# Second graph layer: the linear attention's fold put beside the last 20 groups of edges, and its finish regrouped over seven and two tiles

## What is computed

```python
xn = _layernorm(x, axis=-1)
x = x + _L1_gnn_ref(xn, edge_index, ...) + _L1_mix_ref(xn[None], ...)[0]

# _L1_gnn_ref, the end of it
denom = jax.ops.segment_sum(ex, dst, num_segments=N)
alpha = ex / (denom[dst] + 1e-16)
out = jax.ops.segment_sum(h[src] * alpha[:, :, None], dst, num_segments=N)
return out.reshape(N, H * C) + bias

# _L1_mix_ref: 8 heads of 64
q, k, v = ...          # xn @ w_qkv; k and v normalized per head
dots = jnp.einsum('bhnd,bhne->bhde', k, v)
out = jnp.einsum('bhnd,bhde->bhne', q, dots) * (1.0 / n)
return out @ w_out + b_out
```

## Time and profile before

| | us |
|---|---|
| median of 3 runs | 4831.45 (4831.15 to 4832.38) |
| the profiled execution | 4826.72 |
| its span in the trace | 4825.0 |
| `Stage2`, first DMA issue to the copy's end | 2046.85 to 3200.92 |
| `fold1`, to the first work of `finish1` | to 3219.79 |
| `finish1`, to the end of its last operation | to 3300.94 |

### The profile page before, as it was taken

The page is one execution under the profiler, slowest core; times in us unless marked ns, Lnnn a source line. Parts: engine busy times, 40 slices in busy tenths (PEclk is TensorE's granted clock), DMA queues, the critical chain, the costliest instruction groups (busy, mean ns, idle before and its releaser), DMA issues. The chain is left out here.

```text
span 4825.0 us, 68016 instructions
## 1 busy us (share of the span) xinstructions
PE 3819.0 (79%) x17730; PEld 2381.1 (49%) x17730; DVE 3259.6 (68%) x10150; ACT 2202.3 (46%) x3971; POOL 2816.7 (58%) x2922
## 2 busy tenths in 40 slices
PE   7478789999999999768888888764448888878776
PEld 6344456656665566534444444443424444444444
DVE  7667274645546455488888888876566777777777
ACT  4123222233323223356666666620346666666665
POOL 0355376656656420077777777730477777777775
PEclk9999799999999999989999999886568889998888
DMA  1232311111111100344444444531222222222221
GB/s 60 54 88 64 99 46 34 42 34 37 41 30 40 23 16 1 126 125 138 140 137 136 139 140 140 138 91 32 64 34 39 40 40 44 41 39 40 39 38 28
DMA packets 277159, 323.15 MB, mean 67 GB/s; under 512 B 78502, under 2 KB 232004, under 8 KB 276796
## 3 DMA queue, kind: packets, MB, share of 16 engines
q0 software_dynamic: 105328, 175.77, 16.5%
q1 hardware_dynamic: 171468, 143.20, 10.1%
HBM read 288.85 MB, written 29.89 MB: 66 GB/s over the span
## 5 line engine op out<-in xcount | busy, mean ns | idle before, releaser
L2716 POOL DMA_INDIRECT st_rows<-tabr,router_rsrc x1072 | 1022.2, 954 | 334.7 <-issue 322.1
L1392 POOL DMA_INDIRECT st_rows<-tab,graph_gsrc x748 | 741.8, 992 | 499.8 <-PE st_pe L1415 299.0
L2134 POOL DMA_INDIRECT all_XT<-tab,graph_gsrc x880 | 867.6, 986 | 272.2 <-issue 252.5
L1645 ACT ACTIVATE st_h<-st_ph,st_shift,st_scale 128x448 f32<-128x448 f32 x448 | 324.4, 724 | 757.4 <-PE st_ph L1503 757.2
L2164 PE MATMUL st_po<-all_XT,st_hot 128*128 128x264 f32 x1760 | 579.6, 457 | 84.2 <-DVE gat_sum L2317 83.0
L2317 DVE TENSOR_TENSOR gat_sum<-gat_sum,st_po 128x264 f32 x880 | 376.5, 428 | 143.5 <-DVE gat_sum L2317 75.4
L2164 PEld LDWEIGHTS st_po<-all_XT,st_hot 128*128 128x128 f32 x1760 | 297.5, 204 | 288.1 <-DVE gat_sum L2317 176.3
L2761 PE MATMUL st_px<-all_XT,st_w 128*128 128x512 f32 (+1 forms) x832 | 424.0, 659 | 10.7 <-ACT st_hid L2821 10.7
L1732 DVE TENSOR_TENSOR gcn_acc<-gcn_acc,st_pe 128x65 f32 x748 | 166.3, 222 | 381.7 <-PE st_pe L1415 290.7
L2773 PE MATMUL st_py<-st_w,st_hid 128*128 128x256 f32 x1568 | 422.5, 416 | 0.5 <-ACT st_hid L2821 0.5
L2734 PE MATMUL st_pad<-st_adr,st_hott 128*128 x1072 | 121.1, 183 | 346.4 <-DVE st_zd L2887 325.4
(11 more groups left out here) (489 smaller groups left out, 7233.4 us busy)
## 6 DMA issues: line engine op xcount, KB each, us to landing
st_bc<-drowr SPq DMA_DIRECT2D x268, 128.0 KB
st_bc<-drow SPq DMA_DIRECT2D x220, 128.0 KB
st_rows<-tabr,router_rsrc POOLq DMA_INDIRECT x1072
all_XT<-tab,graph_gsrc POOLq DMA_INDIRECT x880
xtd<-tab_xt SPq DMA_DIRECT2D x98, 128.0 KB, 1.9
st_rows<-tab,graph_gsrc POOLq DMA_INDIRECT x748
tab<-gat_sum SPq DMA_DIRECT2D x7, 924.0 KB
all_XT<-xtd SPq DMA_DIRECT2D x49, 128.0 KB
```

The source lines that it names most:

```text
L1392: g.indirect_dma_start(self.rows[:, b, u, :], None, self.R.tab0, bass.IndirectOffsetOnAxis(self.R.gsrc[:, t:t + 1], 0)).then_inc(self.s_ro ...
L1645: a.activation((self.h1, self.h2)[l][:, fb, h * HALF:(h + 1) * HALF], self.ph[:, m % 3, 0:HALF], ACT.Relu, bias=self.shift[:, l, i:i + 1], ...
L2134: g.indirect_dma_start(self.rows[:, b, u, :], None, self.R.tab1, bass.IndirectOffsetOnAxis(self.R.gsrc[:, t:t + 1], 0)).then_inc(self.s_ro ...
L2716: g.indirect_dma_start(self.rows[:, b, u, :], None, self.R.tabr, bass.IndirectOffsetOnAxis(self.R.rsrc[:, t:t + 1], 0)).then_inc(self.s_ro ...
```

## The change

Three things. The fold moves from a phase of its own into `Stage2`, in five steps tied to the loop steps q = 200 (`FOLD`) to 204: DVE copies `pacc` and masks it (step 0), PE multiplies with `wout` (1), DVE copies the product in two operations (2), PE multiplies with `wqt` (3), DVE copies `weff` (4). Its weights are loaded by SP, behind the row of group 200 and behind a wait for the last `keys`, since they take the place of `wkv`; its mask is made by POOL ahead of the first gather of the stage. `fold1` is gone. `finish1` works with longer operations: the product with the reciprocals and the two additions that don't need PE over seven tiles at a time, the addition of the matmul's result over two tiles; it has four PSUM banks of two tiles and three feature buffers, and loads the features of the first iteration before the biases.

```diff
@@ -2027,6 +1976,7 @@
     HALFKV = KV // 2
     FEAT = GH * GC
     PAIRS = HALFKV // P
+    FOLD = 4 * (W + 1)
...
+        K = self.PAIRS
+        old = self.wkv.rearrange("p c n -> p (c n)")
+        self.wqt = old[:, 0:K * D].rearrange("p (k d) -> p k d", k=K)
+        self.wout = old[:, K * D:2 * K * D].rearrange("p (k d) -> p k d", k=K)
+        old = self.kc.rearrange("p k n -> p (k n)")
+        self.m1 = old[:, 0:K * D]
+        self.bd = old[:, K * D:K * D + K * P].rearrange("p (k e) -> p k e", k=K)
+        self.kvsum = old[:, K * D + K * P:K * D + 2 * K * P]
+        assert 2 * K * D <= C * self.KV and K * D + 2 * K * P <= 2 * self.KV
+        self.diag = f.sb("diag", [P, P])
...
@@ -2121,10 +2083,15 @@
             n, b = divmod(q, 4)
             if b == 3 and n + 1 < W:
                 features(n + 1)
+            if q == self.FOLD:
+                s.wait_ge(self.s_kvp, 2 * W)
+                s.dma_start(self.wqt, rows(self.A.m1_wqt)).then_inc(self.s_fw, 16)
+                s.dma_start(self.wout, rows(self.A.m1_wout)).then_inc(self.s_fw, 16)
 
 
 
     def pool(self, g):
+        block_mask(g, Steps(g, self.s_mask), self.diag, HC1)
         for q in range(self.GROUPS):
...
+        def fold(step):
+            K = self.PAIRS
+            if step == 1:
+                t.wait_ge(self.s_fw, 32)
+                t.wait_ge(self.s_bd, K)
+                for k in range(K):
+                    bank = (self.pkv, self.pacc)[k // 2]
+                    mm = t.matmul(bank[:, k % 2 * D:(k % 2 + 1) * D], self.bd[:, k, :], self.wout[:, k, :],
+                                  start=(k % 2 == 0), stop=False, skip_group_check=True)
+                mm.then_inc(self.s_pm, 1)
+            if step == 3:
+                t.wait_ge(self.s_m1, 2)
+                for m in range(C):
+                    for k in range(K):
+                        mm = t.matmul(self.pkv[:, m * D:(m + 1) * D], self.wqt[:, k, m * P:(m + 1) * P],
+                                      self.m1[:, k * D:(k + 1) * D], start=(m == 0 and k == 0), stop=False,
+                                      skip_group_check=True)
+                mm.then_inc(self.s_pw, 1)
...
             scores(q + 3)
             if b == 3 and 1 <= n <= W:
                 outer(n - 1)
+            if q > self.FOLD:
+                fold(q - self.FOLD)
...
+        def fold(step):
+            K = self.PAIRS
+            if step == 0:
+                v.wait_ge(self.s_kv, W)
+                v.tensor_copy(self.kvsum, self.pacc[:, :]).then_inc(self.s_kvs, 1)
+                v.wait_ge(self.s_kvs, 1)
+                v.wait_ge(self.s_mask, 3)
+                for k in range(K):
+                    v.scalar_tensor_tensor(self.bd[:, k, :], self.kvsum[:, k * P:(k + 1) * P], 1.0 / N, self.diag[:, :],
+                                           ALU.mult, ALU.mult).then_inc(self.s_bd, 1)
+            if step == 2:
+                v.wait_ge(self.s_pm, 1)
+                v.tensor_copy(self.m1[:, 0:2 * D], self.pkv[:, :]).then_inc(self.s_m1, 1)
+                v.tensor_copy(self.m1[:, 2 * D:4 * D], self.pacc[:, :]).then_inc(self.s_m1, 1)
+            if step == 4:
+                v.wait_ge(self.s_pw, 1)
+                v.tensor_copy(R.weff[:, :, :].rearrange("p c d -> p (c d)"), self.pkv[:, :])
...
@@ -2380,8 +2386,8 @@
                 variance(n - 1)
             if b == 2 and 1 <= n <= W:
                 weigh_values(n - 1)
-        v.wait_ge(self.s_kv, W)
-        v.tensor_copy(R.kvsum[:, :], self.pacc[:, :])
+            if q >= self.FOLD:
+                fold(q - self.FOLD)
...
         den = f.sb("den", [P, W, GH])
-        xt = f.sb("xt", [P, 2, TPI, C, P])
-        po = f.ps("po", [P, 2, 512])
-        s_x = [f.sem(f"x{k}") for k in range(2)]
-        s_w, s_st, s_o, s_m, s_b, s_a, s_m2 = (f.sem(n) for n in ("w", "st", "o", "m", "b", "a", "m2"))
+        xt = f.sb("xt", [P, 3, TPI, C, P])
+        po = f.ps("po", [P, 4, 2, D])
...
             @block.sync
             def _(s):
-                s.dma_start(bias[:, 0, :], spread(A.gat_bias[0])).then_inc(s_w, 16)
-                s.dma_start(bias[:, 1, :], spread(A.m1_bout[0])).then_inc(s_w, 16)
                 for i in range(ITER):
-                    if i >= 2:
-                        s.wait_ge(s_o, TPI * (i - 1))
-                    s.dma_start(xt[:, i % 2].rearrange("p j c t -> p j (c t)"),
-                                R.xtd[TPI * i:TPI * (i + 1), :, :].rearrange("j p d -> p j d")).then_inc(s_x[i % 2], 16)
+                    if i >= 3:
+                        s.wait_ge(s_o, TPI * (i - 2))
+                    s.dma_start(xt[:, i % 3].rearrange("p j c t -> p j (c t)"),
+                                R.xtd[TPI * i:TPI * (i + 1), :, :].rearrange("j p d -> p j d")).then_inc(s_x[i % 3], 16)
+                    if i == 0:
+                        s.dma_start(bias[:, 0, :], spread(A.gat_bias[0])).then_inc(s_w, 16)
+                        s.dma_start(bias[:, 1, :], spread(A.m1_bout[0])).then_inc(s_w, 16)
 
             @block.tensor
             def _(t):
-                for i in range(ITER):
-                    t.wait_ge(s_x[i % 2], 16 * (i // 2 + 1))
-                    for j in range(TPI):
-                        n = TPI * i + j
-                        if n >= 2:
-                            t.wait_ge(s_b, n - 1)
+                for k, ns in enumerate(pairs):
+                    if k >= 4:
+                        t.wait_ge(s_b, k - 3)
+                    for n in ns:
+                        i, j = divmod(n, TPI)
+                        if j == 0:
+                            t.wait_ge(s_x[i % 3], 16 * (i // 3 + 1))
                         for c in range(C):
-                            mm = t.matmul(po[:, n % 2, 0:D], xt[:, i % 2, j, c], R.weff[:, c, :], start=(c == 0),
-                                          stop=(c == C - 1))
+                            mm = t.matmul(po[:, k % 4, n - ns[0], :], xt[:, i % 3, j, c], R.weff[:, c, :],
+                                          start=(c == 0 and n == ns[0]), stop=False, skip_group_check=True)
                         mm.then_inc(s_o, 1)
 
             @block.vector
             def _(v):
                 st = Steps(v, s_st)
 
+                def scale(i):
+                    a = R.gat[:, TPI * i:TPI * (i + 1), 0:GH * GC].rearrange("p t (h c) -> p t h c", c=GC)
+                    d = den[:, TPI * i:TPI * (i + 1), :]
+                    v.tensor_tensor(a, a, d.unsqueeze(3).to_broadcast([P, TPI, GH, GC]), ALU.mult).then_inc(s_m, 1)
+
+                def gather(i):
+                    v.wait_ge(s_m, i + 1)
+                    x = R.X[:, TPI * i:TPI * (i + 1), :]
+                    v.tensor_tensor(x, x, R.gat[:, TPI * i:TPI * (i + 1), 0:GH * GC], ALU.add).then_inc(s_p, 1)
+                    v.wait_ge(s_p, 2 * i + 1)
+                    v.tensor_tensor(x, x, bias[:, 0, :].unsqueeze(1).to_broadcast([P, TPI, D]), ALU.add).then_inc(s_p, 1)
+
+                def mixed(k):
+                    n, m = pairs[k][0], len(pairs[k])
+                    v.wait_ge(s_o, n + m)
+                    v.wait_ge(s_p, 2 * ((n + m - 1) // TPI) + 2)
+                    x = R.X[:, n:n + m, :]
+                    v.tensor_tensor(x, x, po[:, k % 4, 0:m, :], ALU.add).then_inc(s_b, 1)
+
                 st.then(v.tensor_scalar(den[:, :, :], R.gat[:, :, GH * GC:GROW], 1e-30, None, ALU.max))
                 st.then(v.reciprocal(den[:, :, :], den[:, :, :]))
+                scale(0)
                 v.wait_ge(s_w, 32)
                 st.then(v.tensor_tensor(bias[:, 0], bias[:, 0], bias[:, 1], ALU.add))
-                for n in range(W):
-                    a2 = R.gat[:, n, 0:GH * GC]
-                    a3 = a2.rearrange("p (h c) -> p h c", c=GC)
-                    v.tensor_tensor(a3, a3, den[:, n, :].unsqueeze(2).to_broadcast([P, GH, GC]), ALU.mult)\
-                        .then_inc(s_m, 1)
-                    xj = R.X[:, n, :]
-                    v.wait_ge(s_o, n + 1)
-                    v.tensor_tensor(xj, xj, po[:, n % 2, 0:D], ALU.add).then_inc(s_b, 1)
-                    v.wait_ge(s_m, n + 1)
-                    v.tensor_tensor(a2, a2, bias[:, 0], ALU.add).then_inc(s_m2, 1)
-                    v.wait_ge(s_m2, n + 1)
-                    v.wait_ge(s_b, n + 1)
-                    v.tensor_tensor(xj, xj, a2, ALU.add).then_inc(s_a, 1)
+                done = 0
+                for i in range(ITER):
+                    if i + 1 < ITER:
+                        scale(i + 1)
+                    gather(i)
+                    while done < len(pairs) and pairs[done][-1] < TPI * (i + 1):
+                        mixed(done)
+                        done += 1
...
-                R.kvsum = h.sb("kvsum", [P, 512])
                 R.adl = h.sb("adl", [P, W, 2 * GH])
                 table1(nc, R, A)
                 with Phase(nc, "st2") as f:
-                    Stage2(f, nc, R).run()
-                fold1(nc, R, A)
```

(1 more changed line is left out.)

52 lines of the change are left out of this document (7 added, 45 removed).

## The result

The changed kernel takes 4797.69 us where the kernel before takes 4831.45 us (medians). The ratio is 0.9932, with a 95% interval from 0.9916 to 0.9947, or 33.8 us less. One of the five executions of the changed kernel took 13132.67 us, for a reason that no trace shows, and the ratio leaves it out. Two later comparisons gave 0.9931 (0.9916 to 0.9946) and 0.9933 (0.9919 to 0.9946). 4801 was predicted. Its profiled span is 4796.9 us against 4825.0, 28.1 less.

A forecast was written before the change was run, and what follows sets the result against it. DVE was taken to bound the finish and the loop steps that take in the fold. The terms 18.5 - 3.4 - 2.0 - 0 - 0.95 + 18.6 gave 30.7 us off 4831.45, about 4801, range 4795 to 4812.

The forecast's parts named there:

- The forecast case: Whole kernel: the changes gain and cost what the summed terms say, 30.7 us less, 4801 us; chance 0.72.
- Part 1: Between Stage2 and the finish: the fold phase of 19.46 us goes, one barrier of 1.0 stays; gain 18.5 us.
- Part 2: The fold's copies and masks on DVE in steps 200, 202 and 204 count in full; loss 3.4 us.
- Part 3: The fold's PE passes in steps 201 and 203: eight hide, sixteen stall DVE; loss 2.0 us, ends 0.2 and 5.
- (a): In the finish: PE bounds it, finish 76 us, kernel 4814 us; chance 0.12.
- Part 4: Weights on SP's queue ahead of group 201's row: the row lands just in time for ACT; price 0.
- (b): In Stage2: the weights on SP's queue make group 201 late by 7 us, kernel 4808 us; chance 0.06.
- Part 5: POOL makes the mask ahead of Stage2's first gather, and the shift passes on; loss 0.95 us, ends 0 and 2.
- Part 6: The finish with longer DVE operations takes 62.5 us in place of 81.15; gain 18.6 us.
- (c): In the finish: PE falls to 1.2 GHz and stays there, finish 102 us, kernel 4843 us; chance 0.03.
- (d): In the finish: longer operations run slower than priced, so it keeps its length, kernel 4819 us; chance 0.04.

The follow-up runs named there:

- finish_only: The kernel before with its old fold phase kept and only the finish new; 5610.75 us against 5632.69 before in slower runs, ratio 0.9958.
- late_weights: The changed kernel with five more 256 KB loads, each waited for and read by nobody, on SP's queue ahead of the weights; 4805.35 us.
- half_passes: The changed kernel with half of the finish's matmul passes left out, two a tile in place of four; its finish took 62.80 us.
- more_passes: The changed kernel with six matmul passes a tile in the finish in place of four; its finish took 72.22 us.

## Why the prediction was right

The forecast case happened, and its sum was right over the changed stretch: 31.2 us measured, 30.7 predicted. Point by point:

- **Part 1** (18.5): the phase is gone and one barrier of 1.07 us stays, gain 18.4. The finish_only run shows the same 19.41 us with the new finish, so this belongs to the phase alone.
- **Part 2** (3.4): 1.54 + 1.20 + 0.6 (step 204 without its stall: 5.08 - 4.48) = 3.34 us. Taking the spacing of DVE's operations as their full price was right, and moving the copies to ACT gave 2.5 of it back, all but the masks (3.34 - 0.82). That eight passes hide held in the changed kernel, and failed by 0.67 us in late_weights.
- **Part 3** (2.0, ends 0.2 and 5): the mechanism was right and the size off. In the changed kernel steps 203 and 204 are 1.43 us longer than two plain ones and the copy (4.83 + 6.16 - 2 x 4.48 - 0.60), and PE's passes, 5.39 us long, set that. In the five profiles at a higher clock the two steps are 0.35 longer, and this is not PE's. What was mis-sized is the price of a pass. Full clock was taken as 0.25 us and 1.2 GHz as 0.49, where passes start 0.216 and 0.427 apart. The old phase's 0.354, used for rival (a), is a mixture: its sixteen passes start 0.427 apart at first and 0.216 at the end.
- **Part 4** (0): right, as ACT's reading of the row at 3105.93 has no DMA wait. The working was too cautious on the loads. The last keys end at 3093.42 + 1.02 = 3094.44 in the changed kernel, and the row lands near 3102.1, 7.7 us later, where 9 to 11 were forecast (3098 to 3100 against 3089.0). late_weights showed 7.4 us of cover, and rival (b) would have needed a row later by more than that.
- **Part 5** (0.95, ends 0 and 2): neither confirmed nor refuted. POOL's first gather is 0.9 us later. DVE's third addition `st_z` comes 31.7 us after the start of the stage in six of the seven profiles with the mask there (32.8 in one), 31.5 before and 31.4 and 31.5 in the two kernels with the mask at group 100. Step 198 starts 1058.3 to 1059.4 us after the stage in those seven, 1059.0 in the mean, and 1057.8 to 1058.5 in the other three, 1058.2 in the mean: 0.8 us, with a scatter of 1.
- **Part 6** (62.5 us): 63.29, with 62.8 to 63.5 in six more profiles with this finish. The slope of 1.035 ns an element was right (pairs 0.60 apart, 1.94 between a scaling and its addition); the waits on an own result cost 0.12 to 0.20 each rather than 0.12, and the tail waits 0.2 for PE. The biases' wait was met at +6.7 us (predicted 7.0).
- The clock in the finish was 0.80 to 0.91, where 1.00 was forecast as its mark. That was wrong and cost nothing: half_passes shows that DVE loses nothing to PE there, and by more_passes PE had 26% in hand at full clock.
- The sum: 0.6 us less than forecast in part 3 and 0.8 more in part 6 nearly cancel, and that is luck. The medians differ by 33.8 us and the stretch by 31.2; no trace gives the other 2.6, which are well inside the interval of the ratio.

**The rivals.** (a) PE as the bound of the finish: excluded by half_passes. The last sign named for it, PE as releaser of most pairs, was absent too: 0.2 us in all. (c) PE at 1.2 GHz: behind the start of the changed kernel's finish the clock fell to it three times, each time at or just behind an idle gap of PE, and never stayed there; with more work PE got more clock, not less. The Trainium skill's page "TensorE: Matmul & The Clock Gate", section "HAM oscillation", has idle gaps throw the clock back. The trace agrees, with the 0.76 to 0.91 of the finishes in which PE idles and the 1.00 of more_passes. But at 1.2 GHz throughout, 28 passes would be 12.0 us against DVE's 8.2, and PE was never there for that long. (d) Long operations: 2.02 us each, no loss by strides or broadcast. The Trainium skill's formula on the page "VectorE: DVE Perf Modes", in the section on the trn2 errata, (N + 151) / 0.96 ns, gives 2.024 us for 1792 elements, which is the measured length. But the next operation starts 1.94 us after the start of such a one where it need not wait, and 0.335 us after the start of a 256-element one of 0.42. So the finish gained 17.9 us (18.6 forecast), where starts as far apart as lengths would have given 9.4 more than the forecast. The section "The DRAIN you can't avoid", which the prediction set against its own spacings, says itself that a next operation that is not held starts earlier, and the trace's spacings agree with that sentence.

## What to carry to other kernels

Price an operation by the distance from its start to the next start on its engine, not by its length, and put the price in full where that engine has no gaps; the same copies cost nothing on an engine that has some, here ACT in place of DVE. Work on PE between its sums is free up to a limit that depends on the clock granted at that moment, so split it in small pieces and count the sums behind it at the lower value too: even eight passes cost 0.67 us once. And look at the first operation of each kind behind a phase's end: 7 us lay there, unmoved by a change on both sides of it, and one throwaway operation placed under other work took them away.
